# A mixture-of-experts layer: rows scattered to sorted places and loaded by slots, in place of one-hot tables and a gather per slot

## The reference

```
xf     = layernorm(x)                                   # 1024 x 256
scores = sigmoid(xf @ gate_w.T)                         # 64 experts
choice = scores + e_bias
groups : 8 groups of 8 experts; score = sum of the best two; the best 4 groups stay
topk   : the 8 best choices of what stays; weight = score / sum(scores) * 2.5
y     += weight * (silu(xf @ Wg.T) * (xf @ Wu.T)) @ Wd.T     for each chosen expert, 176 wide
out    = x + y + shared expert (352 wide, all tokens)
```

## Time and profile before

| | |
|---|---|
| median of 3 runs | 388.62 us (387.45 to 389.07) |
| span of the profiled execution | 389.5 us |
| PE busy / DVE / ACT / POOL | 278.7 / 259.8 / 210.1 / 230.7 us |
| moved by DMA | 64.28 MB |
| chain that ended last, largest parts | PE 31%, DMA 27%, DVE 13% |

### The profile page before, as it was taken

How to read it: one execution, slowest core, us unless ns; L and a number is a source line. 1 busy time by engine, 2 the same in 40 slices (tenths; PEclk the granted TensorE clock), 3 DMA queues, 4 the chain that set the end, 5 groups by cost and what they waited for, 6 DMA issues and landing times.

```text
span 389.5 us, 8382 instructions
## 1 busy us (share of the span) xinstructions
PE 278.7 (72%) x1502; PEld 219.1 (56%) x1503; DVE 259.8 (67%) x815; ACT 210.1 (54%) x507; POOL 230.7 (59%) x221
## 2 busy tenths in 40 slices
PE   0103298589997989977887889879897988869300
PEld 0002174445666977766776778667776866758200
DVE  3999879799016766656566667656675666546696
ACT  1242344037402877667667667766776776647300
POOL 8033402123215687777877877777787778777800
PEclk9999999789759999999999999999999999999755
DMA  7600021004403364447657668887746666599943
GB/s 226 245 0 0 1 78 33 0 0 141 136 0 112 118 202 147 140 139 200 183 175 209 199 220 274 242 270 236 231 158 212 196 207 187 170 335 369 366 136 109
DMA packets 37161, 64.28 MB, mean 165 GB/s; under 512 B 4636, under 2 KB 25148, under 8 KB 37148
## 3 DMA queue, kind: packets, MB, share of 16 engines
q1 hardware_dynamic: 27164, 34.90, 28.7%
q0 software_dynamic: 9984, 29.24, 23.6%
HBM read 49.18 MB, written 14.94 MB: 165 GB/s over the span
## 4 chain that ended last, share of the span: by engine, by line
PE 31%; DMA 27%; DVE 13%; issue 9%; ACT 3%; SPq 2%; POOL 1%; DVEq 1%; POOLq 1%; ACTq 0%
DMA rows<-xfw,gidx 23%; PE bank L1116 9%; PE bank L1160 5%; DVE x L963 4%; PE bank L1091 4%; PE bank L1040 4%; PE bank L1110 3%; PE bank L1028 3%; DMA d_ring<-w_down 2%; DMA early_c<-w_gu 2%; PE bank L1146 2%; DVE gtop L797 1%; ACT early_t L630 1%; SPq L376 1%; POOL planes L525 1%
## 5 line engine op out<-in xcount | busy, mean ns | idle before, releaser
L284 POOL DMA_INDIRECT rows<-xfw,gidx x90 | 99.3, 1103 | 46.2 <-issue 18.9
L525 POOL DMA_INDIRECT planes<-early_cq,sidx x84 | 98.3, 1170 | 25.7 <-issue 15.6
L325 DVE TENSOR_TENSOR gu_lo<-early_c,gu_hi 128x704 fp32r<-128x704 f32 x87 | 77.7, 894 | 42.3 <-ACT gu_hi L321 42.3
L1160 PE MATMUL bank<-d_ring,early_c 88*128 x336 | 88.5, 386 | 0.0
L321 ACT ACTIVATE gu_hi<-early_c 128x704 fp32r x87 | 67.9, 782 | 0.0
L331 DVE TENSOR_TENSOR r_lo<-bank,r_hi 128x256 fp32r<-128x256 f32 x86 | 36.4, 424 | 40.6 <-ACT r_hi L305 39.6
L1160 PEld LDWEIGHTS bank<-d_ring,early_c 88*128 88x128 f32 x336 | 58.5, 191 | 7.9 <-issue 1.3
L1116 PE MATMUL bank<-gu_hi,r_hi 128*128 128x352 f32 x170 | 62.2, 366 | 0.8 <-DVE r_lo L331 0.8
L1110 PE MATMUL bank<-ident,rows 128*128 128x128 f32 x172 | 35.8, 291 | 35.8 <-DMA rows<-xfw,gidx 33.3
L1116 PE MATMUL bank<-gu_hi,r_lo 128*128 128x352 f32 x170 | 55.1, 324 | 0.0
L1116 PE MATMUL bank<-gu_lo,r_hi 128*128 128x352 f32 x170 | 55.0, 323 | 0.0
(11 more groups left out here) (196 smaller groups left out, 354.0 us busy)
## 6 DMA issues: line engine op xcount, KB each, us to landing
early_c<-w_gu SPq DMA_DIRECT2D x37, 352.0 KB, 3.8
d_ring<-w_down SPq DMA_DIRECT2D x36, 176.0 KB
early<-planes SPq DMA_DIRECT2D x3, 1024.0 KB, 8.3
xc<-planes SPq DMA_DIRECT2D x2, 1024.0 KB, 14.7
oh_j_f<-planes SPq DMA_DIRECT2D x2, 1024.0 KB, 15.1
rows<-xfw,gidx POOLq DMA_INDIRECT x90, 3.8
planes<-early_cq,sidx POOLq DMA_INDIRECT x84, 3.9
xc<-x SPq DMA_DIRECT2D x2, 512.0 KB, 4.1
```

The costliest lines, as they stand in the source:

```text
L284: pool.indirect_dma_start(out=rows[:, r, :], out_offset=None, in_=xfw, in_offset=bass.IndirectOffsetOnAxis(ap=gidx[:, r:r + 1], axis=0), b ...
L325: v.tensor_tensor(gu_lo[:, b:b + 1, :], gu_ring[:, bass.ds(nth % R, 1), :], gu_hi[:, b:b + 1, :].bitcast(fp32), ALU.subtract).then_inc(glo ...
L525: pool.indirect_dma_start(out=planes, out_offset=bass.IndirectOffsetOnAxis(ap=sidx[:, place:place + 1], axis=0), in_=y[:, r, :], in_offset ...
L1160: ins = pe.matmul(OB[b][:, 0:H], iT[:, b, s, :], d_ring[:, place, s, :], start=(s == 0), stop=(s == 1))
```

## The change

- The tables `oh_s`, `oh_p`, `oh_j`, `dest`, `maskT`, `idx_tab` and the stages `ranks` and `places` are gone.
- `xf` and the weights `cw` lie side by side in `xw` (rows of 320 floats). When each token's positions `sidx` are known, POOL scatters the rows to their sorted places in the buffer `xs`: 8 ranks (the token's lowest expert first) of 8 chunks, 64 indirect transfers. After the fourth chunk of a rank it waits until the rank before has landed and adds one to `ranks_in`.
- A slot's rows are now 128 consecutive rows of `xs`. ACT issues their load as a plain transfer (`load_rows`), five slots ahead in a ring of eight, and waits before it for `ranks_in` to reach a number that DVE worked out per slot (`window_ge`, `needs`).
- The scaled output `y` is made on DVE, behind `combine` and a wait on `out_ps`. ACT stores four slots at once to `ys`, at the end of a quad, behind a wait for the fourth `y`.
- POOL gathers the outputs back by token: for each rank 8 indirect gathers, when the quads that the rank needs are stored; it adds ranks 0 to 5 to `fin` itself (128x2048 each, `add_rank(k-1)` behind the gathers of rank k). DVE adds the last two.
- SP fills `ys` with zeros at the start (16 transfers of 1 MB); ACT waits for them before its first load.
- The shared expert: the units run before the routing tables where they can, DVE multiplies the last two (`shared_mult`) and adds all eight outputs.

```
+        xw = sb("xw", [P, C, ROW])
+        xf, cw = xw[:, :, 0:H], xw[:, :, H:ROW]
...
             sp.wait_ge(made, MADE)
+            zeros = ys.rearrange("(a p r) h -> a p (r h)", p=P, r=C)
+            for a in range(FILLS):
+                sp.dma_start(zeros[a, :, :], late[:, :]).then_inc(filled, 16)
...
+            def rank_stored(k):
+                pool.wait_ge(rank_st[k % 2], (k // 2 + 1) * C * 16)
+                pool.sem_inc(ranks_in, 1)
...
+            for k in range(TOPK):
+                at = TOPK - 1 - k
+                for c in range(C):
+                    pool.indirect_dma_start(
+                        out=xs, out_offset=bass.IndirectOffsetOnAxis(ap=sidx[:, c, at:at + 1], axis=0),
+                        in_=xw[:, c, :], in_offset=None, bounds_check=ROWS - 1, oob_is_err=True).then_inc(rank_st[k % 2], 16)
+                    if k > 0 and c == HC - 1:
+                        rank_stored(k - 1)
+            rank_stored(TOPK - 1)
...
+            def add_rank(k):
+                pool.wait_ge(back_in[k], C * 16)
+                if k:
+                    pool.wait_ge(pool_sum, k)
+                pool.tensor_tensor(fin[:, :, :], fin[:, :, :], back[k], ALU.add).then_inc(pool_sum, 1)
...
+            for k in range(TOPK):
+                at = TOPK - 1 - k
+                for n in range(2):
+                    stored = pool.value_load(rank_tab[0:1, n, at:at + 1], min_val=16, max_val=16 * QUADS + 32)
+                    pool.wait_ge(y_st[n], stored)
...
+                for c in range(C):
+                    arrived = back_in[k] if k < TOPK - 1 else final_in[c // CL]
                     pool.indirect_dma_start(
+                        out=back[k][:, c, :], out_offset=None, in_=ys,
+                        in_offset=bass.IndirectOffsetOnAxis(ap=yidx[:, c, at:at + 1], axis=0),
+                        bounds_check=QUADS * R * P - 1, oob_is_err=True).then_inc(arrived, 16)
+                if 0 < k <= POOL_SUMS:
+                    add_rank(k - 1)
...
+            def load_rows(start, waited, place):
+                start = act.snap(start, min_val=0, max_val=ROWS)
+                act.wait_ge(ranks_in, (act.snap(waited, min_val=0, max_val=TOPK - 1) & (TOPK - 1)) + 1)
+                act.dma_start(rows[:, place, :], xs[bass.ds(start, P), :]).then_inc(row_in[place], 16)
...
                     weights_high(act, nth, (r + 1) % 2)
-
-                    act.wait_ge(y_st[r], i * 16 + 16)
-                    act.wait_ge(out_ps, i * R + (r + 1))
-                    place = odd * R + r
-                    act.activation(y[:, r, :], OB[r % 2][:, 0:H], ACT.Copy, scale=wcol[:, place:place + 1]).then_inc(y_ok, 1)
+                    load_rows(starts[r], waiteds[r], (odd * R + r + AHEAD) % RING)
+                load_quad(act, nths + starts + waiteds, i + 1, NTH, WAITED)
+                act.wait_ge(y_ok, i * R + R)
+                act.dma_start(ys[bass.ds(i * (R * P), R * P), :].rearrange("(r p) h -> p r h", p=P),
+                              y[:, odd * R:odd * R + R, :]).then_inc(y_st[odd], 16)
...
+                    v.wait_ge(out_ps, i * R + (r + 1))
+                    if r == 0:
+                        v.wait_ge(y_st[odd], pair * 8 + 16)
+                    v.tensor_scalar(y[:, place, :], OB[r % 2][:, 0:H], rows[:, place, bass.ds(expert + H, 1)], None,
+                                    ALU.mult).then_inc(y_ok, 1)
                     weights_low(v, nth, (r + 1) % 2, i * R + (r + 4))
```

More of the change, by code:

```diff
@@ L263, in loop_over_quads @@
                             with eng.If(i < quads):
-                                quad(i, n)
+                                quad(i, n, pair)
         def load_gu(eng, e, r):
@@ L312, in four_registers, with load_quad @@
             return [eng.alloc_register(f"{name}{r}") for r in range(R)]
-        def load_quad(eng, registers, quad, numbers_only=False):
-            part = quad_tab[0:1, bass.ds(quad, 1), (1 if numbers_only else 0):2, :]
+        EXPERT, NTH, START, WAITED = range(4)
+        def load_quad(eng, registers, quad, first, last):
+            part = quad_tab[0:1, bass.ds(quad, 1), first:last + 1, :]
             eng.load(registers, part.rearrange("p q a r -> p (q a r)"))
@@ L529, in _ @@
-            loop_over_quads(pool, quads, quad)
-            for r in range(R):
-                pool.wait_ge(row_in[r], quads * 16 + (32 if r < 2 else 16))
+                        out=back[k][:, c, :], out_offset=None, in_=ys,
[3 more added lines that the diff above has]
+                    add_rank(k - 1)
         @block.scalar
@@ L609, in _ @@
                 weights_high(act, nth, f)
+            for f in range(2):
+                load_rows(first_starts[f], first_waiteds[f], f)
             for f in range(2):
@@ L617, in _, with quad @@
             weights_high(act, nth, 0)
-            def quad(i, odd):
+            for f in range(2, AHEAD):
+                load_rows(first_starts[f], first_waiteds[f], f)
+            def quad(i, odd, pair):
                 for r in range(R):
@@ L961, in _ @@
-            for k in range(TOPK - 1):
-                v.wait_ge(back_in[k], 16)
+            v.wait_ge(pool_sum, POOL_SUMS)
+            for k in range(POOL_SUMS, TOPK - 1):
+                v.wait_ge(back_in[k], C * 16)
                 step(v.tensor_tensor(fin[:, :, :], fin[:, :, :], back[k], ALU.add))
@@ L1099, in _ @@
             logits(1)
-            between = {"u2": [counts], "d0": [cumulate], "u3": [slot_experts, ranks], "d3": [places]}
-            for what in SHARED[1:]:
-                (shared_gate_up if what[0] == "u" else shared_down)(int(what[1]))
-                for routing in between.get(what, []):
-                    routing()
+            for u in range(1, UNITS - 2):
+                shared_gate_up(u)
+            counts()
+            shared_gate_up(UNITS - 2)
+            cumulate()
+            slot_experts()
+            needs()
+            shared_gate_up(UNITS - 1)
+            for c in range(2):
+                shared_down(c)
+            tops()
+            for c in range(2, C):
+                shared_down(c)
             def turn_rows(r, b):
```

503 lines of the change are left out of this document (217 added, 286 removed).

## The result

The changed kernel takes 402.25 us in the median of 4 runs (397.31 to 405.77), the kernel before 388.85 us beside it (387.45 to 390.48): ratio 1.026 (95% interval 1.018 to 1.034). It is slower by 3%. Executions of one kernel fall into a faster and a slower state, and every ratio here is taken from runs in the faster one alone, while the medians are of all runs. Run again on another chip it took 402.51 us, 1.035 (1.023 to 1.047). Forecast were 376 us. The profiled execution has a span of 399.4 us, against 377 in the sum.

A forecast was written before the change was run, and what follows sets the result against it. POOL's gather and scatter per slot were taken to set the pace (2.85 us). Forecast: 129.7 + 158 + 19 = 306.8, quad 17 landed at 311, + 59 = 370, final landing, addition and output to 377, median 376; range 362 to 386 (0.50).

The forecast's parts named there:

- The start of the rows: Before the loop: scatters from about 79.2, 36 at 1.37 us, rank four announced at 128.5; slot 4's down matmuls end at 129.7.
- The zero fill: SP's 16 MB of zeros, from about 6 us: takes 45 to 74 us, costs nothing unless it lasts beyond 95.
- the end of the quad: On ACT: table load (0.9 us at most), wait for fourth `y`, store issue; PE waits some 0.3 us for the next silu.
- the term of 2.36 us: Time per slot in the loop, bounds 2.27 and 2.85; 67 slots from slot 4 to slot 71 make 158 us.
- The rest of the loop: Added to the slots up to quad 17's end: PE's clock 2 us, weights 6, POOL additions 11; then store and landing about 4.5.
- The additions: POOL's 128x2048 additions, 4.5 us each, hold DVE's low weights; three before quad 17's end at 3.6 us make 11 us.
- The end: After quad 17: 32 transfers, three additions and waits, 59 us; then landing 2.8, DVE's last addition 0.7, output 3.3.
- The third: Rival: ACT or DVE, not PE, holds the loop's slot above 2.55 us; at 2.7 the time is 399 us; chance 0.12.
- The others: Rivals: POOL quick, 345 us (0.20); POOL slow, no gain from 1.56 us per transfer (0.09); loads wait for landings, 409 us (0.03).
- the second rival: POOL's 68 indirect transfers on the path are slow: 381 us at 1.44 each, 398 at 1.7; chance 0.09 past 1.56.

## Why the prediction was wrong

**The start of the rows: right in its sum, by luck.** Two errors cancelled. The scatters begin at 80.22 (predicted 79.2), and the 36th starts at 127.30, so (127.30 − 80.22)/35 = 1.345 us for each (predicted 1.37). Slot 4's down matmuls are late and end at 130.3 (predicted 129.7). But the row load of slot 8, the first line here, is issued at 125.19, before the 36th scatter, and not near 128:

```profile
125.19 0.34 ACTq L568 DMA_DIRECT2D rows<-xs  x1
...
126.90 0.44 ACTq L613 DMA_DIRECT2D ys<-y  x1
127.60 0.38 ACT L601 ACTIVATE early_c<-bank 88x256 f32<-88x256 f32 x1 [3.25 <-issue]
...
128.26 2.07 PE L1130 MATMUL bank<-d_ring,early_c 88*128 x4 [2.56 <-ACT early_c L601]
```

In other slots such a load starts 0.17 to 0.61 us into `weights_high` (0.29 where they stand at 195.15 and 194.86). Here `weights_high` began at 123.56: it waited 1.0 to 1.5 us, not five. Slot 4 is 128.26 − 123.17 − 2.27 = 2.8 us late, some 1.3 for the rank and some 1.5 for the end of quad 0. The announcement was two scatters earlier than I had counted, and the unpriced quad's end made up for it. Why it was earlier wasn't tested. The zero fill was over in time, and no row load waited for it; from 6 to 50 us the queues moved:

```profile
6.00:50.00 44.00, 9.05 (x44) 5.51 (x45) 37.95 (x85) 14.89 (x46) 12.24 (x10) 1.00 1.00 412
```

**The step that failed: the end of the quad.** The prediction put it at "PE waits for that silu some 0.3 us" and took 2.36 us per slot. It had the parts: "a table load of 12 registers (0.31 for four; 0.9 at most), the wait for the fourth `y`, and one more issue". What it got wrong is the room for them, and with it the term of 2.36 us. It compared sums ("Before, ACT held 2.27 with `y` on it, so even unhidden this fits", said of the row load's issue) where the place counts. These instructions stand behind `weights_high`, with 0.25 us left to the next `iT`. The table load alone took 0.79. Measured by the steps from slot 21 to 44: of four quads two take 10.46 us, one 10.75 and one 11.08, in the mean 10.69, against 4 × 2.36 = 9.44. (These longer turns are also in the kernel with the later store. I put them down to the loop's own branches; that wasn't tried.) If all of the 67 slots are like these, this is 67/4 × 1.25 = 20.9 us of the 22 by which the sum failed up to there.

**The rest of the loop.** From the end of slot 4's down matmuls to that of slot 71's it took 324.5 − 130.3 = 194.2 us. 67/4 × 10.69 = 179.0; the remaining 15.2 stand for clock, weights, late rows and additions, for which the sum had 19. From there to the first gather of rank 4 it was 333.0 − 324.5 = 8.5 us, not 4.5: the addition at 321.42 held `y`. So 0.6 + 20.9 − 3.8 + 4.0 = 21.7, against the measured 333.0 − 311.3.

**The additions: the mechanism was right, the size so for two of three.** Predicted were three before quad 17's end, 3.6 us each, 4.5 us on POOL. Measured: three, 4.53 to 4.56 each on POOL, of which the first cost the loop nothing and the other two 3.0 to 4.1 each. The greater error was one of judgement. I counted them as a price and never asked what the kernel would be without them; they are the larger of the two shares. The Trainium skill (SBUF — State Buffer, the section on the two sides of SBUF) was borne out for this side: `gu_lo`, with two inputs in SBUF, was held; `y`, which reads PSUM, took its 0.48 us at 322.36, inside the addition.

**The end: right.** 59 + 7 = 66 us were predicted from the landing of quad 17's store to the end, 66.4 measured, with POOL idle by issue alone.

**The rivals.** The third came true: "ACT, with loads, a wait for the fourth `y` and stores in order ... holds the slot above 2.36 + 12.6/67 = 2.55 us; at 2.7 the time is 399". The quads' mean is 10.69/4 = 2.67 us and the span 399.4. I gave it 0.12. Its part on the fourth `y` was second to the table load while that stood, and became first when that was gone. The others did not: the 0.30 us between two transfers stayed, scatters and gathers kept their pace, and inside the loop PE waited for rows only once, for 2.56 us. One reading in the second rival was wrong: 255 to 295 (0.68) wasn't the busiest stretch of the loop before. From 224 to 263 the DMA share was 0.81, and POOL's transfers took 1.05 us each there, so the argument stood all the same.

**Not settled.** The version with the quad's end altered saved 12.1 us before rank 4, not 20.9. In the even stretch from slot 20 to slot 44 its six quads take 60.1 us in place of 64.0, so 0.65 us is won at each where the excess was 1.25: the moved instructions cost where they went (slots with a store or a table load took 2.4 to 2.9 us). From slot 44 to the first gather of rank 4 it takes 91.5 us in place of 92.3: there the altered end saves almost nothing. How much of that is weights, how much late rows and how much the additions wasn't separated, so for that part the 20.9 us stay an extrapolation.

## What to carry to other kernels

Before an instruction is given to an in-order engine, measure the gap at its exact place in that engine's order, not the engine's idle time over the iteration: 0.25 us was left here. An addition that is free by its own engine's account may be dear where it locks another engine: ask of each such addition what the kernel is without it, and where in the loop it falls: one that fell on a wait cost nothing here. Where the same queue ends the kernel (here 32 gathers), work before it is worth something only as far as it starts that queue earlier.

## What the runs showed of the hardware

- A register load of 12 from a table took 0.79 us on ACT, one of four 0.31. The Trainium skill (DMA: Bandwidth & Descriptors, the section on latency) gives some 600 ns as the floor of such a load; the measurement decides.
- The issue of a plain transfer on ACT (0.34 us) overlapped the ACTIVATE that ran before it.
- An indirect gather from HBM took 1.01 us on POOL alone and 2.02 (the first 2.91) beside 128x2048 additions of DVE with two inputs in SBUF; with the additions moved away it was 1.01 again for nearly all. The Trainium skill (SBUF — State Buffer, the section on who interferes with whom) infers that such an operation does not stop the writing of descriptors. The runs here speak against that for indirect transfers, which take their indices from SBUF.
- After each hole that an addition made in PE's work, the down matmuls of one or two slots took 1.7 to 2.1 us in place of 1.03 (granted clock 0.50 from 332 to 336). For the addition at 321.42 the slow steps behind it, 4.48 and 3.36 us in place of 2.37 and 2.27, add 3.2 us to the hold of `gu_lo`, which was 3.1 (3.98 in place of 0.88).
